# The circulant filters of a four-layer kernel as 64x64 tiles, with their edge rows in an operand of their own

## The reference

```
x = conv3x3(feature_map, conv_w) + conv_b
x = batch norm of x, times gamma, plus beta
x = relu(x)
grad_x, grad_y = circular 3x3 filters of x (by FFT: filt_x, filt_y)
second_xx, second_yy = the same filters once more (circular 5x5 in sum)
curvature = second_xx + second_yy + square(grad_x) + square(grad_y)
            - 2.0 * grad_x * grad_y + x
```

## Time and profile before

| | |
|---|---|
| median of 3 runs | 2373.32 us (2372.58 to 2376.8) |
| profiled execution | 2379.39 us, span 2377.6 us |
| busy: TensorE, VectorE, ScalarE, POOL | 1984.7, 1207.3, 1137.8, 185.8 us |
| filter stage, first to last filter matmul | 288.0 to 738.0 us |

### The profile page before, as it was taken

The page is one execution under the profiler, slowest core; times in us unless marked ns, Lnnn a source line. Parts: engine busy times, 40 slices in busy tenths (PEclk is TensorE's granted clock), DMA queues, the critical chain, the costliest instruction groups (busy, mean ns, idle before and its releaser), DMA issues.

```text
span 2377.6 us, 85390 instructions
## 1 busy us (share of the span) xinstructions
PE 1984.7 (83%) x38916; PEld 1407.6 (59%) x38916; DVE 1207.3 (51%) x2300; ACT 1137.8 (48%) x1986; POOL 185.8 (8%) x131
## 2 busy tenths in 40 slices
PE   3787599999997899989898999995468888886966
PEld 2454344444444777777777777773365655655766
DVE  3455234444445555555555555552376666542535
ACT  0111335666664655555565555552466667741210
POOL 1000000000001000000000000001323333120000
PEclk9888799999998999999999999997768989985755
DMA  6766735669545334444443444446335653296798
GB/s 134 190 155 137 142 72 142 161 161 214 165 126 175 62 63 81 70 70 82 70 81 64 83 68 81 68 79 186 78 120 153 170 161 112 73 198 196 163 290 254
DMA packets 610284, 306.13 MB, mean 129 GB/s; under 512 B 418236, under 2 KB 586054, under 8 KB 602566
## 3 DMA queue, kind: packets, MB, share of 16 engines
q1 hardware_dynamic: 599376, 283.93, 51.8%
q10 hardware_dynamic: 10560, 16.93, 2.9%
HBM read 172.28 MB, written 128.54 MB: 127 GB/s over the span
## 4 chain that ended last, share of the span: by engine, by line
PE 65%; SPq 9%; DVE 7%; ACT 7%; DMA 6%; issue 5%; ACTq 0%; POOL 0%; DVEq 0%
PE ps L644 12%; PE ps L685 12%; PE ps L764 11%; PE ps L692 7%; PE ps L723 7%; PE ps L748 6%; SPq L455 5%; DMA arena<-xcl 4%; ACT arena L954 3%; PE ps L803 3%; SPq L360 2%; ACT arena L1042 2%; DVE arena L1494 1%; PE ps L825 1%; PE ps L885 1%
## 5 line engine op out<-in xcount | busy, mean ns | idle before, releaser
L1416 DVE TENSOR_TENSOR arena<-arena 128x1024 f32<-128x1024 f32 (+1 forms) x308 | 350.6, 1160 | 236.3 <-ACT arena L1034 235.6
L748 PE MATMUL ps<-arena 62*64 62x108 f32 x11008 | 339.8, 257 | 89.3 <-DMA arena<-xcl 56.5
L748 PEld LDWEIGHTS ps<-arena 62*64 62x64 f32 x11008 | 292.4, 134 | 129.9 <-issue 33.8
L1034 ACT ACTIVATE arena<-ps 128x1024 f32<-128x1024 f32 (+1 forms) x308 | 297.4, 982 | 144.5 <-PE ps L723 144.1
L1042 ACT COPY arena<-ps 128x864 f32<-128x864 f32 x258 | 222.3, 880 | 265.3 <-PE ps L764 240.2
L723 PE MATMUL ps<-arena 63*64 63x128 f32 (+1 forms) x9504 | 325.8, 270 | 25.8 <-ACT arena L1034 13.4
L954 ACT ACTIVATE arena<-arena,nmr,rstd 128x128 f32<-128x128 f32 x752 | 295.2, 512 | 31.9 <-DVE nmr L1230 31.9
L685 PE MATMUL ps<-arena 128*128 128x512 f32 x640 | 289.2, 598 | 15.3 <-ACT arena L968 15.3
L723 PEld LDWEIGHTS ps<-arena 63*64 63x64 f32 x9504 | 280.3, 135 | 32.6 <-issue 17.0
L764 PE MATMUL ps<-arena 64*64 64x384 f32 (+1 forms) x3168 | 262.7, 478 | 1.5 <-issue 1.5
L685 PEld LDWEIGHTS ps<-arena 128*128 128x128 f32 x640 | 120.8, 190 | 168.7 <-issue 168.7
(11 more groups left out here) (135 smaller groups left out, 1825.7 us busy)
## 6 DMA issues: line engine op xcount, KB each, us to landing
arena<-xcl SPq DMA_DIRECT2D x688, 60.0 KB, 2.7
x_dram<-arena SPq DMA_DIRECT2D x16, 2048.0 KB, 7.3
arena<-x_dram SPq DMA_DIRECT2D x16, 2048.0 KB, 15.5
arena<-l_dram SPq DMA_DIRECT2D x32, 1024.0 KB, 13.7
xcl<-arena SPq DMA_DIRECT2D x8, 3072.0 KB, 10.9
arena<-in_x SPq DMA_DIRECT2D x32, 512.0 KB, 10.0
y_dram<-arena ACTq DMA_DIRECT2D x64, 256.0 KB
arena<-in_x SPq DMA_DIRECT2D x16, 1024.0 KB, 16.1
```

The costliest lines, as they stand in the source:

```text
L748: mm = pe.matmul(ps[T2 * j:T2 * j + T2, bank + t, STEPS * uu:STEPS * uu + STEPS], xs[T2 * t:T2 * t + C + LANES, e, j, u, :], own[T2 * t:T2 ...
L1034: nc.scalar.activation(own, raw_op, ACT.Tanh).then_inc(fill_tanh, 1)
L1416: nc.vector.tensor_tensor(own, own, d, ALU.add).then_inc(op_done, 1)
```

## The change

- Each 128x128 circulant matmul becomes 64x64 ones: the diagonal blocks of `circ`, on the four quadrants of the array. So that the two off-diagonal quadrants have work too, odd channels lie in `yp` with their image halves swapped (`y_in` loads them so), and their outputs are written to the other half of PSUM's partitions. A pair p of chunks (8 channels: even ones to the first bank, odd ones to the second) is done in one go, in both filters.
- What the diagonal blocks miss are the four image rows over each seam. They come from `edge`, an operand with 20 rows for each half (4 rows for each of 5 column shifts), and `w_edge`, its weights: one more 64x64 group for each filter. `edges_in` fills `edge` with ten copies from SBUF to SBUF for each half of the channels, issued by POOL once relu is through; SyncE makes `w_edge` once with 16 small copies.
- y goes straight into `yp`, of which there are three now, and relu works in place.
- `place_tap` moves from SyncE's queue to POOL's, one or two taps an image in images 0 to 5.
- VectorE adds by pairs, and shift and scale of the group norm stand after the first pair.

```diff
-            def filter5(h, n):
-
-                pe.wait_ge(relu_done, 4 * h + n // 2 + 1)
-                after(pe, c5_used, 8 * h + n - 1)
-                for d in range(5):
-                    m = pe.matmul(ps[:, n % 2, :], circ[:, d, :], yp[h % 2][:, 4 * n:4 * n + 4, 4 - d:4 - d + W], start=d == 0, stop=d == 4)
-                m.then_inc(c5_mm, 1)
+            def filters(h, p, kernel, first, shifts, bank):
+
+                for d in range(shifts):
+                    for s in range(2):
+                        for half in range(2):
+                            rows, to = slice(T2 * half, T2 * half + T2), T2 * ((half + s) % 2)
+                            pe.matmul(ps[to:to + T2, bank + s, :], circ[rows, first + d, rows],
+                                      yp[h % 3][rows, 8 * p + s:8 * p + 8:2, 4 - d:4 - d + W], start=d == 0, stop=False)
+                for s in range(2):
+                    for half in range(2):
+                        rows, to = slice(T2 * half, T2 * half + 20), T2 * ((half + s) % 2)
+                        c = 8 * (p % 2)
+                        m = pe.matmul(ps[to:to + T2, bank + s, :], w_edge[rows, kernel, :], edge[p // 2][rows, c + s:c + 8:2, 0:W], start=False, stop=True)
+                return m
+
+            def filter5(h, p):
+
+                pe.wait_ge(relu_done, 4 * h + p + 1)
+                if p % 2 == 0:
+                    pe.wait_ge(edge_loaded[p // 2], 160 * (h + 1))
+                after(pe, c5_used, 8 * h + 2 * p)
+                filters(h, p, 0, 0, 5, 0).then_inc(c5_mm, 2)
+
+            def filter3(h, p):
+
+                after(pe, c3_sq, 8 * h + 2 * p)
+                filters(h, p, 1, 5, 3, 2).then_inc(c3_mm, 2)
...
+            def y_in(b):
+
+                own = yp[b % 3][:, :, YPW - W:YPW].rearrange("p (c s) w -> p c s w", s=2)
+                src = image(y_dram, b).rearrange("h (c s) w -> s h c w", s=2)
+                for s in range(2):
+                    for half in range(2):
+                        rows, at = slice(T2 * half, T2 * half + T2), T2 * ((half + s) % 2)
+                        sp.dma_start(own[rows, :, s], src[s, at:at + T2]).then_inc(y_loaded[b % 3], 16)
...
+            sp.wait_ge(circ_made, 1)
+            sp.wait_ge(edge_clear, 1)
+            for half in range(2):
+                for d in range(8):
+                    at = T2 * half + 4 * (d % 5)
+                    sp.dma_start(w_edge[at:at + 4, d // 5, :], circ[T2 - 4:T2, d, T2:P]).then_inc(edge_made, 16)
...
+            def edges_in(b, k):
+
+                pool.wait_ge(relu_done, 4 * b + 2 * k + 2)
+                if b:
+                    pool.wait_ge(c3_mm, 8 * (b - 1) + 4 * k + 4)
+                n = EDGE - 4
+                src = yp[b % 3][:, 16 * k:16 * k + 16, :].rearrange("p c w -> p (c w)")
+                dst = edge[k].rearrange("p c w -> p (c w)")
+                for half in range(2):
+                    last = T2 * (1 - half) + T2 - 4
+                    for d in range(5):
+                        pool.dma_start(dst[T2 * half + 4 * d:T2 * half + 4 * d + 4, 0:n], src[last:last + 4, 4 - d:4 - d + n]).then_inc(edge_loaded[k], 16)
...
+            PLACE_AT = ((0,), (1, 2), (3,), (4, 5), (6,), (7, 8))
+            pool.wait_ge(y_loaded[0], 64)
+            edges_in(0, 0)
+            edges_in(0, 1)
+            pool.wait_ge(zero_stored, 16 * ZEROS)
+            pool.wait_ge(op_taken, 16 * TAPS)
+            for h in range(B + 1):
+                if h:
+                    phase_ends(h - 1)
+                if h + 1 < B:
+                    edges_in(h + 1, 0)
+                    edges_in(h + 1, 1)
+                if h < len(PLACE_AT):
+                    for j in PLACE_AT[h]:
+                        place_tap(j)
+                if h == B - 1:
                     pool.wait_ge(x1_stored[0], 16 * (B // 2))
                     nc.gpsimd.memset(w_op, 0.0).then_inc(op_zero, 1)
...
+                for p in range(4):
+                    if h < B:
+                        curvature(h, p)
+                        squared(h, p)
+                    if p == 0 and h:
                         group_shift(gn1, h - 1)
                         group_scale(gn1, h - 1, t)
```

More of the change, by code:

```diff
@@ L247, in phases @@
             return part(at, XROW).rearrange("p (f u c) -> p f u c", f=PHASES, u=NU)
[L249 to L255, removed]
+        xt = [planes(0), planes(22912)]
+        yp = [planes(4096, YPW), planes(8320, YPW), planes(27008, YPW)]
+        edge = [part(12544 + EDGE * n, EDGE).rearrange("p (c w) -> p c w", w=YPW) for n in range(2)]
+        xn1 = [phases(16768), phases(31232)]
+        sqr = part(37376, 2048).rearrange("p (q u c) -> p q u c", q=2, u=NU)
+        sq = part(39424, 2 * NPX).rearrange("p (a n) -> p a n", a=2)
+        circ = part(40448, 8 * P).rearrange("p (a n) -> p a n", a=8)
+        w_edge = part(48076, 2 * T2).rearrange("p (a n) -> p a n", a=2)
         w_op = part(0, STEPS * T2).rearrange("p (s l) -> p s l", l=T2)
@@ L310, in four_layers @@
         bn_dev, bn_mat, bn_ready = (once(n) for n in ("bn_dev", "bn_mat", "bn_ready"))
-        xt_loaded, yt_loaded, x1_stored, xn1_stored, norm_stored = (two(n) for n in (
-            "xt_loaded", "yt_loaded", "x1_stored", "xn1_stored", "norm_stored"))
+        xt_loaded, x1_stored, xn1_stored, norm_stored, edge_loaded = (two(n) for n in (
+            "xt_loaded", "x1_stored", "xn1_stored", "norm_stored", "edge_loaded"))
+        y_loaded = [once(f"y_loaded{i}") for i in range(3)]
+        circ_made, edge_clear, edge_made = (once(n) for n in ("circ_made", "edge_clear", "edge_made"))
         relu_main, relu_done, c5_mm, c3_mm, c3_sq, c5_used, c3_used = (once(n) for n in (
@@ new lines, in filter5 @@
+            def filter5(h, p):
[7 more added lines that the diff above has]
+                filters(h, p, 1, 5, 3, 2).then_inc(c3_mm, 2)
+            pe.wait_ge(edge_made, 16 * 16)
+            for h in range(B):
+                for p in range(4):
+                    filter5(h, p)
+                    if p == 0 and h:
+                        group_means(gn1, h - 1)
+                    filter3(h, p)
+                    if p == 0 and h:
@@ L699, in _ @@
                         group_vars(gn1, h - 1)
-                    filter3(h, n)
-                    if n == 0 and h:
-                        group_means(gn1, h - 1)
             group_means(gn1, B - 1)
@@ L1398, in _ @@
                     group_deviations(gn1, h - 1, t)
-                for n in range(8):
-                    if n == 1 and h:
+                for p in range(4):
+                    if h < B:
+                        curvature(h, p)
+                        squared(h, p)
+                    if p == 0 and h:
                         group_shift(gn1, h - 1)
@@ L1404, in _ @@
                             half_norm(B - 1)
-                    if h < B:
-                        curvature(h, n)
-                    if n in (4, 5) and h:
-                        for q in (2 * n - 8, 2 * n - 7):
+                    if p == 2 and h:
+                        for q in range(4):
                             channel_sums(h - 1, q)
```

116 lines of the change are left out of this document (58 added, 58 removed).

## The result

| | changed kernel | kernel before, same chips |
|---|---|---|
| median | 2439.04 us (5 runs) | 2376.8 us (5 runs) |
| ratio | 1.0253, 95% interval 1.0228 to 1.0278 | |

The change makes the kernel slower by 2.5%; 2338 us was forecast, with 2406 as the upper end of its range. One of the five runs, at 3569 us, had TensorE at about half pace (the operator stage's matmuls of the earlier trace rows were busy for 553 us instead of 263) and stands outside the comparison. "After" is this profile from here on.

A forecast was written before the change was run, and what follows sets the result against it. TensorE, fully busy in the filter stage, was taken as the bound. Start 306 + 36.2 + 51.0 + 270 + 39.3 = 702.6 against 738.04 won 35.4 us: 2344.0 profiled, 2338 as median, range 2303 to 2406.

The forecast's parts named there:

- TensorE's part: Filter stage: four 64x64 quadrants run side by side, 442 ns a group; 35.3 us an image instead of 55.1.
- The rival in which the halves exclude each other: Filter matmuls: two halves writing one PSUM bank can't run together, 884 ns a group; 140 us lost, 2513; chance 0.04.
- The clock: Start of each filter5: after idle, TensorE comes back at a granted clock of 0.50, charged 3.0 us.
- POOL's price: Issuing one edge or operator copy on POOL costs 1.1 us; wrong if issues stand over 1.3 or under 0.8 apart.
- POOL is cheap: Rival on POOL's issues: 0.44 to 0.74 us each, 49 to 50 us an image, 2307 to 2313 us; chance 0.17.
- The chain up to POOL: Filters, squares, adds, relu, normalise, then POOL: phase ends done at S + 40.0, ten edge copies issued at S + 51.0.
- The step that failed: Landing of the edge copies before the next filter5: 3 us, from 2.7 us for 60 KB pieces; period 54.0 us.
- covered, by 2 us: SyncE's next x load: lands 20 us behind the store's issue, S + 60, while VectorE wants it at S + 62.
- VectorE waits for x: Sign of being wrong, in the filter stage: VectorE stands waiting for the x load, which the forecast held covered.
- The start: Before the first filter5: 16 edge-weight issues behind the x load at 0.43 us each; filter5 at 306, 18 us late.

The follow-up runs named there:

- e7: Changed kernel with SyncE issuing the x load of two images on ahead of the store of the phases, not behind it: 2386.6 us, ratio 1.004.
- e2: Changed kernel without edge copies or waits for them, the edge matmuls reading a tile of zeros: 2334.2 us, ratio 0.980.
- e14: Changed kernel with each of the ten edge copies cut to its first quarter, same queue, place and number: 2349.7 us, ratio 0.989.
- e8: Changed kernel with first edge copies ahead of phase ends, edge weights issued by ScalarE, x load ahead of the store: 2350.4 us, ratio 0.988.
- e13: Changed kernel with the edge copies issued by ScalarE's queue instead of POOL's: 2395.7 us, ratio 1.006.
- e12: Kernel before the change, with the x load issued ahead of the store of the phases: 2377.6 us, ratio 0.9995.
- e10: Changed kernel with each edge copy cut into rows of 512 B instead of four runs of 8432 B: 2440.4 us, ratio 1.026.

## Why the prediction was wrong

By its own steps, S being the start of filter5 of an image (422.88 in the trace of after; the next starts at 487.70):

- **TensorE's part** was right in mechanism and nearly in size. Four quadrants side by side, both halves into one bank: the distance from a filter5 pair to the filter3 behind it is 5.48 us at full clock (forecast 5.3), from there on 3.76 (3.5). The rival in which the halves exclude each other is refuted; it needed a group of 884 ns, and ten groups of filter5 take 4.53 us. The timeline of TensorE at full clock, after:

```profile
335.19 4.53 PE L689 MATMUL ps<-arena 64*64 64x512 f32 x40
339.65 1.09 PE L695 MATMUL ps<-arena 20*64 20x512 f32 x8
340.67 2.81 PE L689 MATMUL ps<-arena 64*64 64x512 f32 x24
343.41 1.09 PE L695 MATMUL ps<-arena 20*64 20x512 f32 x8
344.43 1.09 PE L689 MATMUL ps<-arena 64*64 64x512 f32 x8
```

- **The clock** was right in kind: behind the wait the granted clock is 0.50 until 492 and 1.00 from 494, and filter5 takes 6.74 us instead of 4.53, 2.2 us more (forecast 3.0). A second slow one (6.63 us at 505.00) follows the wait for x, which the forecast did not have.
- **POOL's price** was mis-sized on the safe side: 0.52 us an issue, not 1.1, and so outside the 0.8 to 1.3 that the prediction gave itself. That is the condition of the rival "POOL is cheap", whose 2307 to 2313 us did not come, because neither rival nor forecast had the landing right.
- **The chain up to POOL** was nearly right: phase ends done at S + 41.2 (forecast S + 40.0), of which 4.7 us are a wait of VectorE for x that the forecast did not have; ten copies issued at S + 46.4 (S + 51.0).
- **The step that failed**: "an edge copy moves 34 KB and shares the engines with bulk transfers, so 3". The last of the ten had landed 18.5 us after the last issue, S + 64.8 instead of S + 54.0. The bulk was named, and then the price was taken near that of a row of another kind of transfer, which tells nothing of 5 MB beside it. The period came out only 10.8 us too short because two errors ran against each other: 15.5 us too little for the landing, 5.9 too much for the issues, and 1.2 of delay before them.
- **The same step seen from the other side**: the x load "covered, by 2 us" from a landing of 20 us behind the store. It took 39 us, S + 80.7, and the 6.3 us that VectorE waits are in the loop (e7: 50 us). "VectorE waits for x" was one of the prediction's own signs of being wrong. The forecast let the bulk slow nothing and nothing slow the bulk.
- **The start**: the 16 issues behind the x load, priced at 0.43 us each, took 25.7 us, so 323.6 and not 306.

By images the sum closes: 17.6 us more at the start, 3.7 in image 0, 8.3 in image 1, 10.6 to 13.1 in each of images 2 to 6 and 6.6 in image 7 are 94.5 us, and 2338 + 94.5 = 2432.5, against 2439.

What the runs show of the cause: without the copies the change gains 2% (e2), with a quarter of their bytes 1.1% (e14), and with nothing less but another order 1.2% (e8). So the loss is one of order and of DMA traffic, and not of the tiles. Shown is that the edge copies, as POOL issues them, slow the x load, and that at a quarter of their bytes they do not; not shown is how. All edge copies of an image are 0.66 MB beside some 9 MB of bulk, and from 479 to 494 us, with both under way, the DMA engines were used at 28 to 43%:

```profile
474.00:479.00 5.00, 0.00 (x0) 0.00 (x0) 1.48 (x8) 0.98 (x5) 4.15 (x9) 0.50 1.11 188
479.00:484.00 5.00, 0.00 (x0) 0.00 (x0) 0.00 (x0) 0.00 (x0) 5.00 (x9) 0.50 0.43 53
484.00:489.00 5.00, 1.30 (x8) 0.61 (x12) 0.00 (x0) 0.00 (x0) 3.16 (x6) 0.50 0.28 60
489.00:494.00 5.00, 5.00 (x36) 1.56 (x28) 0.00 (x0) 0.00 (x0) 0.00 (x0) 0.68 0.31 74
```

The last two columns of these windows (after) are the DMA share and GB/s: 53 to 74 GB/s, where 188 moved just before. Parted by queue (packets, MB, share of 16 engines; q0 is that of POOL's issues, q1 that of SyncE's with the x load in it), first 480 to 492 us, then 494 to 500:

```profile
q0 software_dynamic: 531, 0.44, 22.8%
q1 hardware_dynamic: 458, 0.23, 7.2%
```

```profile
q1 hardware_dynamic: 2019, 1.05, 91.1%
q0 software_dynamic: 30, 0.00, 0.4%
```

While the last edge copies are under way SyncE's queue nearly stands still, and when they are through it fills the engines. And in e13, from 463 to 469 us, the first copies of ScalarE's queue (q10) run with no bulk beside them, and keep 3.6 of the 16 engines busy:

```profile
q10 hardware_dynamic: 33, 0.14, 22.7%
```

Both fit with copies that go from four partitions to four and so use a few of the engines, while the rest of the x load waits for those; but the trace has no times of single engines, and a copy spread over more partitions was not tried. Whether POOL's queue has a share in it stays open too (e13 lies between).

## What to carry to other kernels

A small transfer that a matmul waits for must be priced in the traffic that the same event releases: look up what else is issued at that moment, and issue the small one ahead of it. Here that order, with the x load ahead of the store, was worth 86 us, more than twice the gain of 35 us that was forecast for the whole change. Before calling a load "covered" by 2 us, follow what stands behind its reader in program order: VectorE's wait for x also held the shift of the group norm, and so closed a loop in which each image paid. When a matmul is made faster, the slack of every load beside it goes: the order of SyncE's queue was worth nothing in the kernel before (e12) and 50 us in the changed one (e7).

## What was unexpected of the hardware

- Copies of 33 KB between four partitions and four, twenty of them an image, lengthened a 2 MB load from 19.4 to 33.7 us (median) when POOL issued them, in pieces of 8432 or of 512 B (35.6 us, e10); at a quarter of the bytes they did not (18.9 us, e14).
- A DMA instruction of SyncE can hold its engine far longer than its own work: 27.85 us for two loads behind a 3 MB store, 10.6 us for the first of the 16 weight copies behind a load, where the median of the 16 is 0.58.
- An issue on POOL took 0.52 us, the larger of the scattered ones 0.61, less than the 0.71 that the same ones took on SyncE in the kernel before (medians).
